# A graph network kernel: column order and output stride of the identity matmuls in layer 1

## What is computed

```
sender, receiver = x[src], x[dst]
h = relu(concat([sender, receiver, edge_attr_32]) @ W1 + b1)       # 200000 x 128
aggregated = segment_sum(h @ W2 + b2, dst) / max(degree, 1)        # 12500 x 64
x = layernorm(x + aggregated + x @ Wn + bn)
```

## Time and profile before

| | |
|---|---|
| median of three timed runs | 5320.2 us |
| profiled execution, whole time | 5303.53 us |
| its span | 5301.8 us |
| mean granted TensorE clock | 0.608 |
| POOL busy | 3508.6 us, 66% of the span |
| DVE busy | 2196.3 us, 41% |
| PE busy | 1752.7 us, 33% |
| ACT busy | 1728.1 us, 33% |
| identity matmuls of layer 1 | 784 records, 741.4 us |
| edge matmuls of layer 1 | 784 records, 496.6 us |

### The profile page before, as it was taken

One profiled execution on the slowest core, in us unless ns is written; L12 is line 12 of the kernel. 1 busy time (PEld: TensorE's weight loads), 2 busy tenths in 40 slices (PEclk: granted clock), 3 DMA queues, 4 the chain that ended last, 5 costly groups with the idle time before them and its releaser, 6 DMA issues.

```text
span 5301.8 us, 22035 instructions
## 1 busy us (share of the span) xinstructions
PE 1752.7 (33%) x3727; PEld 739.0 (14%) x3747; DVE 2196.3 (41%) x2960; ACT 1728.1 (33%) x1393; POOL 3508.6 (66%) x3562
## 2 busy tenths in 40 slices
PE   4630000000000000003464455454555555555544
PEld 2210000000000000002231111111111111111113
DVE  3453222222222222225543465454555555455445
ACT  2422111111111111112233454454554555445431
POOL 5567777777777777775547566666666666666634
PEclk7965555555555555555556677676766767677665
DMA  4025333333333333332333344444444444444432
GB/s 165 7 79 170 107 107 107 107 107 107 106 107 107 106 107 106 107 102 85 98 104 116 120 160 140 135 151 133 153 151 140 146 151 152 133 152 150 134 104 79
DMA packets 202250, 635.79 MB, mean 120 GB/s; under 512 B 70347, under 2 KB 72848, under 8 KB 157808
## 3 DMA queue, kind: packets, MB, share of 16 engines
q1 hardware_dynamic: 88624, 457.72, 23.2%
q0 software_dynamic: 113344, 177.81, 14.3%
q10 hardware_dynamic: 256, 0.00, 0.0%
HBM read 335.07 MB, written 300.32 MB: 120 GB/s over the span
## 4 chain that ended last, share of the span: by engine, by line
POOL 29%; another core or an unknown queue 22%; issue 21%; DVE 15%; PE 10%; ACT 1%; DMA 1%; DVEq 1%; ACTq 0%; SPq 0%; POOLq 0%
POOL edge_arena L499 28%; DVE node_arena L1330 11%; PE ps L644 10%; POOL edge_arena L511 1%; ACT node_arena L822 1%; DVE edge_arena L1363 0%; DVE node_arena L1348 0%; DVE ps L1227 0%; POOL edge_arena L597 0%; DVE node_arena L1340 0%; DMA table<-node_arena 0%; DVE node_arena L1228 0%; DMA node_arena<-recv_term 0%; DVE node_arena L1224 0%
## 5 line engine op out<-in xcount | busy, mean ns | idle before, releaser
L597 POOL DMA_INDIRECT edge_arena<-table1s,ix x1568 | 1482.3, 945 | 816.4 <-issue 507.3
L499 POOL DMA_INDIRECT edge_arena<-table,ix x1440 | 1496.8, 1039 | 498.6 <-issue 498.6
L1330 DVE TENSOR_TENSOR_SCAN node_arena<-ps,node_arena 128x510 f32<-128x510 f32 (+1 forms) x980 | 945.5, 1038 | 97.2 <-issue 73.3
L644 PE MATMUL ps<-node_arena,ident 128*128 128x512 f32 x784 | 741.4, 1102 | 356.6 <-issue 247.8
L644 PE MATMUL ps<-w1e_bd,edge_terms 128*128 128x512 f32 x784 | 496.6, 782 | 760.7 <-issue 436.2
L644 PE MATMUL ps<-we_bd,edge_terms 128*128 128x32 f32 x392 | 93.6, 403 | 1885.1 <-issue 1495.1
L1363 DVE TENSOR_TENSOR edge_arena<-edge_arena,ps 128x1024 f32<-128x1024 f32 x196 | 238.6, 1218 | 1001.1 <-remote 806.2
L1170 DVE TENSOR_TENSOR score<-edge_arena,node_wide 128x128 f32<-128x128 f32 x49 | 18.6, 380 | 1466.6 <-DMA edge_arena<-table,ix 1451.0
L951 ACT ACTIVATE node_arena<-edge_arena 128x2048 f32<-128x2048 f32 x98 | 374.6, 3822 | 676.4 <-issue 670.5
L930 ACT ACTIVATE node_arena<-node_arena 128x2048 f32<-128x2048 f32 x98 | 375.3, 3830 | 523.3 <-DMA node_arena<-recv_term 450.7
L834 ACT ACTIVATE ps<-expo 128x128 f32<-128x128 f32 x49 | 13.8, 281 | 1402.8 <-issue 1244.6
(11 more groups left out here) (199 smaller groups left out, 1845.9 us busy)
## 6 DMA issues: line engine op xcount, KB each, us to landing
recv_term<-zeros SPq DMA_DIRECT2D x98, 1024.0 KB
node_arena<-recv_term SPq DMA_DIRECT2D x98, 1024.0 KB
rows<-edge_arena SPq DMA_DIRECT2D x98, 1024.0 KB
rows<-edge_arena SPq DMA_DIRECT2D x49, 1152.0 KB
edge_arena<-table,ix POOLq DMA_INDIRECT x1568
edge_terms<-e32g_d SPq DMA_DIRECT2D x98, 256.0 KB
edge_arena<-table1s,ix POOLq DMA_INDIRECT x1568
edge_terms<-e16g_d SPq DMA_DIRECT2D x49, 256.0 KB
```

The lines of the kernel that those rows point to most:

```text
L499: pool.indirect_dma_start(G0[slot][:, u, :], None, table0, bass.IndirectOffsetOnAxis(ap=ix[slot][:, u:u + 1], axis=0)).then_inc(gathered0[ ...
L597: pool.indirect_dma_start(G1[slot][:, u, :], None, table1s, bass.IndirectOffsetOnAxis(ap=ix[slot][:, u:u + 1], axis=0)).then_inc(gathered1 ...
L644: return pe.matmul(out_, lhsT, rhs, start=start, stop=stop)
L1330: last = scan(F[:, lo:hi], hold[:, 0:hi - lo], F[:, lo:hi], 0.0, ALU.mult, ALU.add)
```

## The change

In the second loop of `edge1` the columns of an identity matmul were taken edge by edge: 128 features of one edge, then those of the next, which matches the order in PSUM. Now they are taken feature by feature: the four edges of a feature, which lie side by side in the feature-major tile, then those of the next feature. The output is addressed so that each element lands where it did before: the four edges of a feature are 128 elements (512 bytes) apart in the bank. The number of instructions, their order on every engine, their waits and the values that are summed are the same.

```
                 for g in range(4):
-                    recv = F1_f[XF1[r]][:, :, 1 + 4 * g:5 + 4 * g].rearrange("p f t -> p t f")
-                    last = mm(ps[:, 2 + g, :].rearrange("p (t f) -> p t f", f=HID), ident[:, :], recv, False, True)
+                    recv = F1_f[XF1[r]][:, :, 1 + 4 * g:5 + 4 * g]
+                    last = mm(ps[:, 2 + g, :].rearrange("p (t f) -> p f t", f=HID), ident[:, :], recv, False, True)
                     if g % 2:
                         last.then_inc(edge1_mm, 1)
```

## The result

| | before | after |
|---|---|---|
| median of the timed runs | 5319.4 us (4 runs, 5312.4 to 5334.5) | 5361.4 us (4 runs, 5345.0 to 5365.7) |
| profiled execution (span) | 5303.5 (5301.8) us | 5345.0 (5343.3) us |
| mean granted TensorE clock | 0.608 | 0.609 |
| PE busy | 1752.7 us | 1595.0 us |
| identity matmuls, busy | 741.4 us | 538.3 us |

So this measurement puts the changed kernel 0.75% above the kernel before: slower by more than the 0.3% that I had called the limit. The first figure stands as the result, but neither of the others bears it out, so most of it is probably not the change's.

What follows compares the result with a forecast made beforehand. POOL's gather bursts bound it: rounds of 60 us of gathers, 4.9 us to the late add, some 6 us to release. Profiled 5303.5 minus 1 is 5302.5, with 16.7 for timed runs 5319 us; range 5240 to 5460.

Steps and rivals of the forecast that it cites:

- The pass of 0.88 us: Identity matmuls of layer 1: a pass goes from 0.907 to 0.88 us, eight passes -0.2 us a chunk.
- rival 1: Output stride of the identity matmuls is cheap, passes run with the clock at 0.68 us: say 5275 us, chance 0.22.
- bounds a factor of four apart: Identity pass with strided output: 0.43 us at full and 0.85 at half clock from below, 1.71 us from above.
- The rounds of three stay: POOL's gather rounds in layer 1 stay three chunks with one late, 70 us a round, 23.5 us a chunk.
- late semaphores: PE's semaphore for DVE's adds comes 14 and 23 us late in each round's third chunk, following POOL's burst.
- The reading side: Strided SBUF read holds identity passes at 0.907 us; four neighbours in at most two 16-byte lines would free it.
- The matmuls aren't in the sum of a round: A round is 60 us of gathers, 4.9 to the late add, some 6 to release; identity matmuls add nothing.
- The cover: POOL's burst hides PE's growth by 3.5 us behind the first chunk and 6.8 us behind the second.
- four chunks in 80 + 10.6 us: POOL's rounds grow to four chunks with only the fourth late: 22.6 us a chunk for 23.5, 88 us saved.
- the likeliest case: Whole kernel with a pass of 0.80 to 1.33 us: 5319 us, spanning 5300 to 5340, chance 0.50.
- rival 4: Slow reads by PE cause the late semaphores, which go with them: about 4980 us; chance within 0.07 for two rivals.
- rival 3: Costly output stride makes POOL wait, short gaps end the late semaphores: about 5120 us; chance within 0.07 for two rivals.

Runs made afterwards that it cites:

- e7: The changed kernel with its feature-by-feature reads but a contiguous PSUM output, so terms land on wrong columns: 5332.2 us, 1.0019 times the kernel before.
- e2: The kernel before with identity passes of 384 columns in place of 512, slow strided reads kept: 5330.8 us, ratio 1.0007.
- e10: The kernel before with SP's load of receiver terms cut from 16 to 2 edge columns a chunk: 5340.9 us, ratio 1.0013.
- e3: The kernel before with one semaphore increment of two after the fourth identity matmul in place of two increments of one: 5347.8 us, ratio 1.0040.
- e12: The changed kernel with two POOL memsets (2048 and 1024) after each chunk's gathers, 3.1 us of pause: 5242.3 us, 0.9832 times the kernel before.
- e13: The kernel before with two POOL memsets (2048 and 1024) after each chunk's gathers, 3.1 us of pause: 5228.1 us, ratio 0.9814.
- e8: The changed kernel as it is, measured again with twelve runs: 5336.7 us, 1.0013 times the kernel before.
- e15: The changed kernel as it is, measured once more on another chip job with twelve runs: 5334.4 us, 1.0005 times the kernel before.
- e6: The kernel before with one POOL memset of 1024 columns after each chunk's gathers, 0.95 us of pause: 5338.6 us, ratio 1.0021.
- e4: The kernel before with POOL waiting after each chunk's gathers until they have landed: 5447.3 us, ratio 1.0225.
- e9: The kernel before with 8 of the 16 gathers of a chunk: 4517.5 us, ratio 0.8473.
- e5: The kernel before with one POOL memset of 2048 columns after each chunk's gathers, 2.0 us of pause: 5304.6 us, ratio 0.9969.

## Why the prediction was wrong, point by point

**The pass of 0.88 us: wrong.** This is the first step that failed: "my estimate is that the strided output costs about what the strided input cost". The strided output costs nothing (0.493 and 0.853 us with it, 0.494 and 0.853 without it in e7), so the pass fell to 0.493 at full and 0.853 at half clock, and a chunk's eight to some 3.9 to 6.8 us from 7.3. The mechanism that held was rival 1's, to which I gave 0.22. I had kept the forecast near the middle of bounds a factor of four apart, though no row gave a reason for any cost on the writing side; on the reading side one did.

**The rounds of three stay: wrong, and through this step the pass reached the profile.** I wrote that "the release follows the end of POOL's burst and not the length of the matmuls", that "POOL's rounds stay 70 us", and that I would be wrong altogether if the length of the matmuls moved the late semaphores. It did. The changed kernel runs in rounds of four with two late chunks, 96 to 97 us, 24.1 us a chunk, and e2, which only shortens the passes, does the same. Of the kernels that keep the long passes and have no pauses, before has sixteen rounds of three in its profile, e10 twenty and seven of four, and e3 almost nothing but rounds of three. Against the mixed rounds of before this is +0.42 us a chunk and 31.8 us over the stage of the profiled pair. I had also read "in every round two chunks go through PE without delay" off one round, and nine rounds of before say otherwise.

**The reading side: right, with a remainder.** One limit of the strided read is gone with four neighbours in a row. The rule of the 16-byte lines (the Trainium skill, SBUF — State Buffer, Specifications (TRN2)) foretold full speed; at half clock the trace agrees, at full clock the pass is 15% above an edge pass, for a reason that no run isolates.

**The matmuls aren't in the sum of a round: right as a sum.** 203 us of the identity group went, and none of it came out at the end, in three measurements and again in e12 against e13. The cover held: POOL's bursts hide a chunk's PE work. What a shorter pass changes is which chunks fall late, and that isn't a term of this sum.

**Rival 1's sum, 5275 us: wrong.** It let the rounds go from three chunks to four, as they did, but with only the fourth late: "four chunks in 80 + 10.6 us". The third and the fourth are late, and the round takes 97 us. The trace of before had such rounds, in rows that I hadn't read; POOL's starts of two bursts, four chunks apart:

```profile
3290.54 0.94 POOL L597 DMA_INDIRECT edge_arena<-table1s,ix  x1 [10.90 <-ACT ix L804]
...
3387.51 0.94 POOL L597 DMA_INDIRECT edge_arena<-table1s,ix  x1 [16.07 <-ACT ix L804]
```

96.97 us are 24.2 us a chunk, slower than the 23.5 of a round of three. Priced from these, rival 1 would have been 0 to 0.7 us a chunk slower than before, not 0.9 faster: up to 98 x 0.7 = 69 us.

**The time.** 5361 us lies in the range of 5240 to 5460 but outside the 5300 to 5340 of the likeliest case, and on the side to which I gave 0.23. The +36 us of rhythm in the profiled pair follow from the shorter pass through the rounds of four, which every profile of a kernel with a shorter pass shows (after, e2, e7, e8, e15). Why the timed runs of e2, e7, e8 and e15 give only 0.05 to 0.19% where this would be 0.7% stays open. A possible reason is that the kernel before runs in rounds of four more often than its profile shows: that profile has nine of them, and e6, with its long passes and only a small pause, ran in them mostly; e3 and e10 speak against it. But only one profile of before itself exists, whose 5303.5 us lies 15.9 below its median, so this is argued and not shown. What of the 1.0075 is left over I can't attribute; few runs and the chip are candidates. That e8 and e15 came out close to my 5319 us is luck: the pass was far from 0.88 us and the rounds weren't those of the forecast.

**The late updates: what I left unexplained decides the stage.** That they follow POOL's bursts was right, and e4, e9, e12 and e13 show it from four sides; that the slow reads cause them was wrong (rival 4; after and e9). That they would go once POOL has pauses was my rival 3, and it holds for pauses of 3.1 us in every chunk, though the change doesn't bring such pauses; its "short gaps" weren't enough at 2.0 us a chunk (e5), nor at up to 6.8 us after a burst of 60. What inside the chip holds PE's updates back while POOL issues without a pause was not found.

## What to carry to other kernels

Price an unseen cost from the side on which a row gives a reason for it, and ask first whether the engine is on the path at all: here 203 us less of identity matmuls bought nothing. Read the rhythm over a whole stage and not in one round; the other rhythm that a change may lock into often stands in the same trace, with its price. And where a wait has no releaser that the profile can name, test it by loading or unloading the engine whose bursts it follows: a pause of 3.1 us in POOL's row of gathers was worth 1.9%, the tuned matmuls nothing.

## What the runs showed of the hardware that I had not expected

- PE's semaphore updates arrive late, 39 of 41 late chunks of before by 14 to 30 us, while POOL issues indirect DMAs with little pause; in the first chunks, where POOL never stops, the second add comes up to 38.4 us after the first matmul. One update or two for a chunk makes no difference (27.8 and 28.2 us).
- A standstill of POOL of 2.3 to 6.8 us, in 17 of 18 cases after a burst of some 60 us, left the chunk next to it late in all 18 (before and after); one of 7.4 us or more did in none of 50. Put after every 20 us of gathers, pauses of 2.0 us don't cure it, 3.1 us do (82 of 82 recorded updates prompt in e13).
- f32 passes of 512 columns with a PSUM output of 512 bytes between elements run as fast as with a contiguous one (0.493 and 0.494 us at full clock, 0.853 at half). With single reads 68 bytes apart a pass took 0.907 us at both 1.2 and 2.4 GHz.
- The same kernel's runs lie as far apart as 5294 and 5359 us, and two measurements of one kernel gave 1.0075 (1.0045 to 1.0104) and 1.0005 (0.9986 to 1.0023): the interval of one measurement of four runs doesn't hold what the next one adds, and no run tells whether that is the chip.
